# An LSTM with residual: the loops of TensorE and VectorE begin at a chunk's fourth step, two calls on zeros go, and three of five waits

## The reference

```python
xW = jnp.einsum('ntd,dk->tnk', x, Wx) + b        # x (4, 512, 256), Wx (256, 1024)
c0 = jnp.zeros_like(h0)                          # h0 = cond_1024 (4, 256)
def step(carry, xw_t):
    prev_h, prev_c = carry
    a = xw_t + prev_h @ Wh                       # Wh (256, 1024)
    i = sigmoid(a[:, 0:H]); f = sigmoid(a[:, H:2*H]); o = sigmoid(a[:, 2*H:3*H]); g = tanh(a[:, 3*H:4*H])
    next_c = f * prev_c + i * g
    next_h = o * jnp.tanh(next_c)
    return ((next_h, next_c), next_h)
out = x + lstm(x, h0, Wx, Wh, b)
```

## Time and profile before

| what | us |
| --- | --- |
| three runs | 1054.12, 1056.75, 1073.64 |
| median of them | 1056.75 |
| the profiled execution | 1052.39 |
| its span, first to last instruction | 1050.3 |
| PE busy | 1029.1 |
| DVE busy | 697.8 |
| ACT busy | 620.2 |

### The profile page before, as it was taken

How to read it: one execution, slowest core, us unless ns; L and a number is a source line. 1 busy time by engine, 2 the same in 40 slices (tenths; PEclk the granted TensorE clock), 3 DMA queues, 4 the chain that set the end, 5 groups by cost and what they waited for, 6 DMA issues and landing times.

```text
span 1050.3 us, 105684 instructions
## 1 busy us (share of the span) xinstructions
PE 1029.1 (98%) x45316; PEld 835.7 (80%) x45316; DVE 697.8 (66%) x4453; ACT 620.2 (59%) x4610; POOL 0.7 (0%) x6
## 2 busy tenths in 40 slices
PE   5999999999999999999999999999999999999997
PEld 4888887888888887888888878888888878888885
DVE  4566666666666666666666666666666666666664
ACT  2466666556666666566666665566666665666664
POOL 0000000000000000000000000000000000000000
PEclk9999999999999999999999999999999999999999
DMA  3000000000000000000000000000000000000000
GB/s 91 5 7 7 6 6 7 6 6 7 6 6 6 6 6 6 6 7 6 6 7 6 6 7 6 6 7 6 6 7 6 6 7 6 6 7 6 6 6 7
DMA packets 32111, 8.76 MB, mean 8 GB/s; under 512 B 31584, under 2 KB 31584, under 8 KB 32096
## 3 DMA queue, kind: packets, MB, share of 16 engines
q1 hardware_dynamic: 31488, 8.41, 3.7%
q10 hardware_dynamic: 608, 0.14, 0.1%
HBM read 6.43 MB, written 2.10 MB: 8 GB/s over the span
## 4 chain that ended last, share of the span: by engine, by line
PE 98%; SPq 1%; issue 0%; DMA 0%; DVE 0%; ACT 0%; DVEq 0%
PE gates L414 28%; PE o_units L431 27%; PE x_acc L406 19%; PE f_units L423 12%; PE x_acc L372 7%; PE gates L380 2%; PE o_units L394 2%; PE f_units L387 1%; SPq L151 1%; DMA wh_raw<-in_L_cond_Wh_dram 0%; SPq L155 0%; DVE wh L237 0%; ACT scan_both L222 0%; DVE wh L234 0%; DVE a_bank L325 0%
## 5 line engine op out<-in xcount | busy, mean ns | idle before, releaser
L414 PEld LDWEIGHTS gates<-wh,h_pad 128*32 128x32 f32 x16384 | 333.1, 111 | 172.2 <-DVE h_pad L343 157.5
L414 PE MATMUL gates<-wh,h_pad 128*32 128x64 f32 x16384 | 425.6, 227 | 1.3 <-DVE h_pad L290 0.9
L216 ACT ACTIVATE tanh_f<-f_units 128x4 f32<-128x4 f32 x1024 | 175.1, 171 | 369.3 <-PE f_units L423 369.3
L423 PE MATMUL f_units<-h_pad,wh 128*32 128x4 f32 x16384 | 368.3, 173 | 0.7 <-issue 0.7
L423 PEld LDWEIGHTS f_units<-h_pad,wh 128*32 128x32 f32 x16384 | 329.1, 111 | 0.7 <-issue 0.7
L431 PE MATMUL o_units<-h_pad,wh_o 128*64 128x4 f32 x8192 | 327.1, 202 | 0.7 <-issue 0.7
L431 PEld LDWEIGHTS o_units<-h_pad,wh_o 128*64 128x64 f32 x8192 | 283.9, 139 | 8.7 <-issue 0.7
L325 DVE STREAM_TRANSPOSE a_bank<-gates 128x64 f32<-128x64 f32 x512 | 136.0, 266 | 163.8 <-PE gates L414 153.1
L406 PE MATMUL x_acc<-wh,zeros 128*32 128x256 f32 x772 | 240.3, 393 | 0.0
L336 DVE TENSOR_TENSOR_SCAN cell<-scan_both 128x12 f32<-128x12 f32 x1024 | 187.0, 183 | 68.0
L225 ACT ACTIVATE tanh_o<-o_units 128x4 f32<-128x4 f32 x1024 | 169.6, 166 | 12.8 <-PE o_units L431 4.5
(11 more groups left out here) (42 smaller groups left out, 258.3 us busy)
## 6 DMA issues: line engine op xcount, KB each, us to landing
x_next<-in_x_dram SPq DMA_DIRECT2D x256, 8.0 KB
x_here<-in_x_dram SPq DMA_DIRECT2D x256, 8.0 KB
out_dram<-y_rows SPq DMA_DIRECT2D x256, 8.0 KB
wx_raw<-in_L_cond_Wx_dram SPq DMA_DIRECT2D x8, 128.0 KB, 3.5
wh_raw<-in_L_cond_Wh_dram SPq DMA_DIRECT2D x8, 128.0 KB, 2.9
bias_raw<-in_L_cond_b_dram ACTq DMA_DIRECT2D x4, 32.0 KB, 3.1
h_rows<-in_cond_dram ACTq DMA_DIRECT2D x4, 1.0 KB
```

Source lines behind the costliest of these rows:

```text
L216: nc.scalar.activation(tanh_f[:, m, :], f_units[m][:, t * N:(t + 1) * N], ACT.Tanh).then_inc(tanh_f_done[m], 1)
L414: last = nc.tensor.matmul(gates[k][q * R:(q + 1) * R, columns], h_stationary(b, t), wh[:, b, q, k * W + columns.start:k * W + columns.stop ...
L423: last = nc.tensor.matmul(bank[q * R:(q + 1) * R, t * N:(t + 1) * N], wh[:, b, q, at:at + R], h_at(b, t - 1), start=False, stop=b == M - 1 ...
```

## The change

The constant LAP_END = 2 is the last step before the loops' new boundary. DVE does steps 0 to 2 of chunk 0 ahead of its loop; one pass is steps 3 to 7 of chunk k and 0 to 2 of chunk k + 1, for k from 0 to 62; steps 3 to 7 of chunk 63 follow it. PE does the same. The turn of the next chunk's x moves from step 2 to step 4. On PE the call on zeros of step 2 goes, and the one behind the injects of step 7; that step waits for `gates_turned[BB]` and `tanh_f_done[1]` alone and no longer for `gates_turned[BA]`, `tanh_f_done[0]` and `x_part_turned`. ACT, POOL and SP keep their programs.

```diff
--- before.py
+++ after.py
@@ -36,7 +36,10 @@
     WIN = R + N
 
     X_PRODUCT_AT = (4, 5)
+    X_TURN_AT = 4
     X_PART_AT = STEPS - 2
+
+    LAP_END = 2
     UNIT_COLUMNS = slice(GC - 4 * R, GC)
 
     ctx = ExitStack()
@@ -311,7 +314,7 @@
                     turn_back(chunk - 1)
                 if not first and t == 1:
                     residual(chunk - 1)
-                if ahead and t == 2:
+                if ahead and t == X_TURN_AT:
 
                     dve.wait_ge(x_next_loaded, (chunk + 2) * (Q * DMA))
                     nc.vector.transpose(x_units[:], x_next[:]).then_inc(x_turned, 1)
@@ -353,12 +356,14 @@
                 hidden(0)
                 hidden(1)
 
-            for t in range(STEPS):
+            for t in range(LAP_END + 1):
                 step(0, t, True, True)
-            with dve.Fori(1, CHUNKS - 1) as k:
-                for t in range(STEPS):
+            with dve.Fori(0, CHUNKS - 1) as k:
+                for t in range(LAP_END + 1, STEPS):
                     step(k, t, False, True)
-            for t in range(STEPS):
+                for t in range(LAP_END + 1):
+                    step(k + 1, t, False, False)
+            for t in range(LAP_END + 1, STEPS):
                 step(CHUNKS - 1, t, False, False)
             turn_back(CHUNKS - 1)
             residual(CHUNKS - 1)
@@ -455,15 +460,12 @@
                 elif ahead and t == X_PART_AT:
                     pe.wait_ge(x_part_made, chunk + 2)
                     keep_busy()
-                elif t < STEPS - 1 or not ahead:
-                    keep_busy()
-                if ahead and t == STEPS - 1:
-                    for k in ROWS:
-                        pe.wait_ge(gates_turned[k], now)
-                    for m in range(M):
-                        pe.wait_ge(tanh_f_done[m], now)
-                    pe.wait_ge(x_part_turned, chunk + 2)
+                elif ahead and t == STEPS - 1:
+
+                    pe.wait_ge(gates_turned[BB], now)
+                    pe.wait_ge(tanh_f_done[M - 1], now)
                     inject_early()
+                elif t != LAP_END:
                     keep_busy()
 
             pe.wait_ge(zeroed, 2)
@@ -475,10 +477,14 @@
             pe.wait_ge(x_part_turned, 1)
             inject_early()
             pe.wait_ge(wh_made, 2 * M)
+            for t in range(LAP_END + 1):
+                step(0, t, True)
             with pe.Fori(0, CHUNKS - 1) as k:
-                for t in range(STEPS):
+                for t in range(LAP_END + 1, STEPS):
                     step(k, t, True)
-            for t in range(STEPS):
+                for t in range(LAP_END + 1):
+                    step(k + 1, t, True)
+            for t in range(LAP_END + 1, STEPS):
                 step(CHUNKS - 1, t, False)
```

## The result

| kernel | runs, us | median |
| --- | --- | --- |
| before | 1054.12, 1056.75, 1062.14, 1073.64 | 1059.45 |
| changed | 1625.96 to 1626.03 (4 runs) | 1626.01 |

The ratio is 1.537, with a 95% interval of 1.530 to 1.545: slower, by 567 us. The rival that gave about 1630 us is what happened.

What follows compares the result with a forecast made beforehand. The recurrence loop from turn to turn was taken as the bound, with PE and DVE holding the chunk edge. 62 edges at 0.29 (18.0 us) plus 1.5 gave 1032.9 to 1037.3, taken as 1035; own range 1028 to 1046, full range 1027 to 1130.

Steps and rivals of the forecast that it cites:

- The rival that gave about 1630 us: PE clock stays at its lower level for most or all chunks, 9.5 us more per chunk; chance 0.20.
- two slow chunks: Slowest earlier run, 21.25 us over the profiled one, read as two edges passed without the clock's rise (2 x 10.71).
- A fall of its own: Clock falls later in the run, in the emptier third step, at the same 9.5 us per chunk; no separate chance.
- The edge: Last step's turn to next chunk's first: 0.31 us gained by dropping PE's call and moving DVE's jump, both needed.
- The chunk: Steady chunk at the higher clock takes 15.57 us, 0.29 less than 15.86.
- The jump at the fourth step: DVE's loop jump, moved ahead of the fourth step's turn, costs 0 with 0.02 us to spare; bound 0.32.
- the jump that is only moved: Rival: 0.1 to 0.3 us of the edge's gain given back per chunk, total 1039 to 1055 us; chance 0.12.
- code loading in every pass: Rival: each pass over the moved jump costs 0.72 us of code fetch, 45 us in all, 1078; chance 0.04.
- The third step's call: Removing PE's call on zeros there gives 0 in the steady part, 0.10 us at most, since the turn waits for h.
- the turn of x: DVE's transpose of x moved from third to fifth step: 0, or 0.03 us moved from one step to another.
- the waits: Two waits instead of five before the injects: only 0.02 us of issue there, nothing gained beyond that.
- The first chunk: At the lower clock, two calls fewer save about 1.5 us: 0.87 at the edge, two thirds of that in the third step.

Runs made afterwards that it cites:

- six of which four were wide: Changed kernel with its calls on zeros given a stationary of 128 columns instead of 32: 1708.43 and 1708.72 us.
- three calls in the seventh step: Changed kernel with three calls on zeros in the seventh step instead of one, none behind the injects or in the third step: 1082.14 and 1083.74 us.
- the call back at the injects: Changed kernel with only the call on zeros behind the injects put back: median 1064.97 us, ratio 1.005 to the kernel before.
- half a call: Changed kernel with a call on zeros of 128 columns instead of 256 behind the injects: 1041.09 to 1100.64 us, median 1067.64.
- bursts: Changed kernel with PE's 63 passes as three times 21 and six calls on zeros ahead of each 21: 1227.04 us.
- the run with early calls: Changed kernel plus four calls on zeros at the start, while PE waits: 1619.96 us (1616.81 to 1623.47).
- the first mended kernel: Changed kernel plus four calls on zeros at the start and four ahead of PE's first and second loop pass: 1028.59 to 1030.22 us, a fifth run 1624.73.
- the moved loops with all calls: Changed kernel with both removed calls on zeros back, plus four calls at the start: median 1039.5 us, two of five runs at 1064.8.

## Why the prediction was wrong, step by step

**The clock.** This is the step that failed. The forecast gave the kernel 0.20 for a clock that stays low for most or all of the run, and put it outside the range. The mechanism was read rightly: the rise in the earlier trace rows fell into the longest stretch without o matmuls, and the change took 0.87 us of calls from it. That two slow chunks account for the slowest run fits as well, though that run has no trace. Its price was right as well: about 1630 us, measured 1626. Wrong was the weight, and with it the forecast's own condition, that the clock is up by the second chunk or one later: all four runs took the time of a clock that never rose, and the one with a trace shows it. Against the rival the prediction put that the injects still stand there, that the stretch is shorter rather than idle, and that six of eight steps keep their filler. The runs show these not to be enough for the rise: six fillers elsewhere, seven with the call in the third step, and six of which four were wide all stayed low in every chunk, and one call more at the injects was enough. Before the run, the rows held more than I used. The only rise that they show is at an edge, and none of the three runs shown was below the profiled execution, where a rise well within the first chunk would have put it. The change thinned out the one place where the rise had been seen. Why the clock rises there, and after three calls in the seventh step, and not elsewhere, these runs do not show; they show which kernels raise it.

**The range.** It left out a case of 0.20 that is 600 us away, because the rest fills 0.80: the other cases had been given more than the rows bore out.

**A fall of its own.** The rival named a fall in the emptier third step. It was seen only in passes through new code or right behind them. With the moved loops the first pass ends in the second chunk's third step, and in four kernels (the call back at the injects, three calls, half a call, bursts) the clock fell between 49.8 and 50.1 us, in the step behind it, each time with an unexplained gap of PE of 0.59 to 0.84 us in the third step. In the kernel before without the third step's call, whose first pass is over at the first edge, the rise at that edge held. In the steady chunks (41 full ones in the run with bursts, 59 and 62 in the two runs that lack only the third step's call) the clock did not fall. But the missing call is not needed for a fall: with all calls in place one came at 19.63 us.

**The edge.** Forecast: 0.31 gained, to 0.44 us from h to turn, both edits needed. Measured with the clock up: the edge at 1.92 us, 0.31 gained; loops and waits without the call's removal 0.07; DVE's h_rows 0.11 us after h where 0.10 was said. What the call's removal would give alone was not seen, as the clock did not hold in that run; so whether DVE's jump would have held the edge then, and both edits were needed, stays open.

**The chunk.** Forecast 15.57 us (0.29 less than 15.86), measured 15.57 in the chunk shown and 15.49 to 15.59 in all.

**The jump at the fourth step.** Forecast 0, with 0.02 us to spare: the pace is 1.92 and the turn 0.44 after h. Right. The rivals of the jump that is only moved and of code loading in every pass fall with it, as the chunks repeat. The step of 2.64 us in the earlier trace rows fits what was seen since: it stands in the last chunk, in code that runs once, with 0.65 us of such a gap in PE.

**The third step's call, the turn of x, the waits.** Forecast 0 each. The third step's call: ratio 1.002 (0.996 to 1.007). The other two have no run of their own. For the waits the prediction read 0.02 us of issue and took that for all there was; the injects start 0.10 us earlier without them, and the edge with its call is 0.06 shorter. It changed nothing in the sum, since h bounds the edge once the call is gone.

**The first chunk.** Forecast 1.5 us less at the lower level, 25.07 against 26.57 measured: 1.50, of which 0.85 at the edge (3.82 to 2.97) and 0.67 in the third step (3.18 to 2.51) where 0.87 and 0.58 were said. This is also why the price of the rival came out so close.

## What to carry to other kernels

Work that looks useless may be what lets the clock rise. Here its place decided, and not its amount alone: of four kernels with seven fillers the two with a call behind the injects rose and the other two never did. Before such a call is taken out, find the moment at which the clock rose and see what stood around it. Raising the clock and keeping it are two things. Here a few calls at the start, where PE waited anyway, and a small one where the rise had been seen, bought the freedom to drop the large ones, and in the five runs made took the spread out.

## What the runs showed of the hardware that was not expected

- PEclk reads 1.00 from the start although the matmuls run at the lower level, in the first 44 us of the kernel before and in all 1624 us of the changed one. It showed 0.50 only after a first rise and fall, as in the windows of the run with early calls. The same 16 o matmuls are the better witness, 0.95 us at 1.2 GHz and 0.56 at 2.4. The Trainium skill warns of it (TensorE: Matmul & The Clock Gate, "Seeing it yourself": the recorded events of the clock gate have been seen to be unreliable and want a cross-check). The trace agrees: 1.00 stands beside 0.95 us.
- A kernel in which PE is marked busy for 99% of 1600 us can stay at 1.2 GHz for all of it, and its loop stays at 2.4 for 976 us (49.38 to 1025.59) in the first mended kernel, once four calls have raised it.
- At the lower level a call on zeros takes 0.87 us of PE and at the higher 0.55, a factor of 1.6. But its two matmuls start 0.43 us apart at the lower level (703.71 and 704.14 in the changed kernel) and 0.22 at the higher (504.04 and 504.26 in the moved loops with all calls), a factor of 2. A whole chunk goes from 25.06 to 15.57 us, 1.6, as at the higher level PE waits for h in a step (0.45 us in the third step of the changed kernel with early calls) and at the lower level does not.
- The first pass through a loop's code costs PE idle stretches, of 0.66 and 0.78 us in the trace above, at the full clock. In none of the 16 traces was there such a stretch over 0.2 us once the steps had begun, except in code that ran for the first time, that of the last chunk included. In the four runs that stayed at the lower level from start to end there was none at all. The Trainium skill (Runtime: NRT & Kernel Launch, "Instruction fetch mechanics") has code fetched in blocks ahead of use and calls the cost mostly hidden; if these stretches are that, here the cost is seen, and beside them the clock fell. What they are was not tested, nor whether they alone made it fall.
